# Order of products in an attention piece: both state products first, then eight quarter-width products

## The chip, the cores and the metric

The kernel runs on one core of a Trainium2 chip. The metric is the device time of one execution in microseconds (us). The kernel before takes 2143.31 us, the median of three runs (2138.61 to 2150.04). Five engines share the work: TensorE (products), VectorE, ScalarE and GpSimd (element-wise work), and SyncE (starts transfers).

## What is computed

Input x has 4 x 1024 tokens of 512 values. Two layers follow each other, each with a normalisation before and after and a sum with its input: a linear attention with decay (16 heads of 32 values, chunks of 128 tokens), and a mixture of 8 experts, 2 per token, with a shared expert. The change touches the attention only, and there the recurrence over chunks:

```python
def step(S, inp):
    qb, kb, vb = inp
    inter = jnp.einsum('bhcd,bhde->bhce', qb * decay_q[None, :, :, None], S)
    scores = jnp.einsum('bhcd,bhed->bhce', qb, kb) * dmask[None]
    intra = jnp.einsum('bhce,bhed->bhcd', scores, vb)
    S_new = lam_c[None, :, None, None] * S + jnp.einsum('bhcd,bhce->bhde', kb * decay_k[None, :, :, None], vb)
    return (S_new, inter + intra)
```

## The kernel before

Tokens are taken in 8 blocks of 512 (two blocks to a sequence), a block in 4 chunks of 128. The 16 heads stand in 4 groups of 4, so a group fills 128 partitions with 4 x 32 values. In each block the attention is a list of pieces with places on a scale (PLACES, OPENING): `QK` and `V` make q, k and v, `Z` (ScalarE) spreads q so that one product gives the scores of four heads, `S` (L741) makes the scores of one group and VectorE masks them into `probs` (L1122), `IP` makes inter + intra, `ST` (L759) the new state, `OUT` the projection.

`IP` is the piece of the change. It exists for each block, chunk and half (two groups), 8 x 4 x 2 = 64 times. For each of its groups it runs a state product, `state` x `qd`, with weights of 128 x 128 (L749), and four quarter-width products, one for each head, with the 128 x 32 weights `v` and the moving operand `probs`; each writes 32 partitions of the output bank (L753). All of it adds up in 256 columns of one PSUM bank, of which ScalarE (L938) and VectorE (L1127) make `attT_hi` and `attT_lo`. These products are plain f32. Large products elsewhere split each operand into a high and a low part and run three products (`three`, L678 to L680).

Block 0 runs its attention alone. From block 1 on, the pieces of attention are mixed with parts of the shared expert (`GA`, `UP`, `DN`) by a list that `schedule` makes: each engine has one fixed order (`ORDER`), and pieces wait for each other by counters (`p_piece`, `a_piece`, `v_piece`). The list holds whole pieces; inside a piece the order is that of the code. The attention ends at about 1290 us of the span; then come the experts and the last block.

Of the kernel before, what the change touches and what calls it, by code (L numbers as in the profile page):

```python
# [16 lines left out]
P = 128  # L17
# [300 lines left out]
def done(engine, *piece):  # L318

    return PLACE[engine][piece]  # L320
# [10 lines left out]
def build(nc, x, w_att, w_ffn, w_gu, w_dn, w_router, b_qk, b_v, b_out, t_mask, t_dq, t_dk, t_lam, t_blk, t_ident,  # L331
# [10 lines left out]
    with ExitStack() as ctx:  # L342
        def sb(name, shape, dt=F32, scope=ctx):
            return scope.enter_context(nc.sbuf_tensor(name, [P] + shape, dt))
# [67 lines left out]
        qd = sb("q_decayed", [G, P], scope=phase1)  # L412
        kd = sb("k_decayed", [D], scope=phase1)
        probs = sb("probsT", [2, GH, P], scope=phase1)
        state = sb("state", [G, P], scope=phase1)
# [186 lines left out]
        def w_landed(a, u):  # L602

            return 32 * ((a - 1) * (NW // WAS) + u // WAS + 1)
# [71 lines left out]
        def three(pe, out_ap, l_hi, l_lo, r_hi, r_lo, start, stop):  # L676

            pe.matmul(out_ap, l_hi, r_hi, start=start, stop=False)  # L678
            pe.matmul(out_ap, l_hi, r_lo, start=False, stop=False)  # L679
            return pe.matmul(out_ap, l_lo, r_hi, start=False, stop=stop)  # L680
# [11 lines left out]
        def pe_bank(pe, piece):  # L692

            old = bank_before(piece)
            if old:
                pe_evicted(pe, old)
            return bank_of(piece)

        def pe_attention(pe, piece):
            kind, a, *args = piece  # L700
            b = pe_bank(pe, piece)
            if kind in ("T1", "T2"):
                c, = args
                pe.wait_ge(a_piece, done("A", "N1", a, c) if kind == "T1" else done("A", "LX", a, c // 2))
                normed = xn2[:, c, 0:D] if kind == "T2" else xin[:, c, :]
                for k in range(KT):
                    mm = pe.transpose(b[:, k * P:(k + 1) * P], normed[:, k * P:(k + 1) * P], ident[:, :])  # L707
            elif kind == "QK":
                m, = args
                if a:  # L710
                    pe.wait_ge(wa_in[m % WAS], w_landed(a, m))
                else:
                    pe.wait_ge(v_piece, done("V", "W", a, m))
                if m == 0:
                    pe.wait_ge(v_piece, done("V", "T1", a, NC - 1))
                for k in range(KT):
                    ks = slice(k * P, (k + 1) * P)
                    mm = three(pe, b, wa_hi[:, m % WAS, ks], wa_lo[:, m % WAS, ks], xa_hi[:, k, :], xa_lo[:, k, :],
                               k == 0, k == KT - 1)
            elif kind == "V":  # L720
                c, = args
                cs = slice(c * P, (c + 1) * P)
                if c == 0:
                    if a:
                        for k in range(KT):
                            pe.wait_ge(wa_in[k], w_landed(a, 8 + k))
                    else:
                        pe.wait_ge(v_piece, done("V", "W", a, 11))
                for k in range(KT):
                    mm = three(pe, b, xa_hi[:, k, cs], xa_lo[:, k, cs], wa_hi[:, k, :], wa_lo[:, k, :],  # L730
                               k == 0, k == KT - 1)
            elif kind == "KT":
                c, = args
                if c == 0:
                    pe.wait_ge(a_piece, done("A", "QK", a, 7))
                for g in range(G):
                    mm = pe.transpose(b[:, g * P:(g + 1) * P], kT[:, g, c * P:(c + 1) * P], ident[:, :])
            elif kind == "S":
                c, g = args
                pe.wait_ge(a_piece, done("A", "Z", a, c, g))  # L740
                mm = pe.matmul(b, kT[:, g, c * P:(c + 1) * P], qz[:, g % 2].rearrange("p h t -> p (h t)"),  # L741
                               start=True, stop=True)
            elif kind == "IP":
                c, half = args
                pe.wait_ge(v_piece, max(done("V", "S", a, c, 2 * half + 1), done("V", "V", a, c), done("V", "KT", a, c)))
                for gl in range(2):
                    g = 2 * half + gl
                    cols = slice(gl * P, (gl + 1) * P)
                    pe.matmul(b[:, cols], state[:, g, :], qd[:, g, :], start=(gl == 0), stop=False,  # L749
                              skip_group_check=True)  # L750
                    for j in range(GH):
                        r = slice(j * HD, (j + 1) * HD)
                        mm = pe.matmul(b[r, cols], v[:, c, g * P + j * HD:g * P + (j + 1) * HD],  # L753
                                       probs[:, g % 2, j, :], start=False, stop=(gl == 1), skip_group_check=True)
            elif kind == "ST":
                c, = args
                for g in range(G):
                    gs = slice(g * P, (g + 1) * P)
                    mm = pe.matmul(b[:, gs], kd[:, gs], v[:, c, gs], start=True, stop=True)  # L759
            elif kind == "OUT":  # L760
                c, = args
                if c == 0:
                    if a:
                        for k in range(KT):
                            pe.wait_ge(wa_in[k], w_landed(a, 12 + k))
                    else:
                        pe.wait_ge(v_piece, done("V", "W", a, 15))
                pe.wait_ge(v_piece, done("V", "IP", a, c, 1))
                for k in range(KT):
                    mm = three(pe, b, oT_hi[:, k, :], oT_lo[:, k, :], wa_hi[:, k, :], wa_lo[:, k, :],  # L770
                               k == 0, k == KT - 1)
            elif kind == "R1":
                pe.wait_ge(v_piece, done("V", "T2", a, NC - 1))
                for k in range(KT):
                    ks = slice(k * R, k * R + P)
                    mm = three(pe, b, rw_hi[:, ks], rw_lo[:, ks], xs_hi[:, k, :], xs_lo[:, k, :],
                               k == 0, k == KT - 1)
            elif kind == "R2":
                pe.wait_ge(a_piece, done("A", "R1", a))
                for c in range(NC):  # L780
                    mm = pe.matmul(b[:, c * R:(c + 1) * R], lgT[0:R, c * P:(c + 1) * P], ident[0:R, 0:R],
                                   start=True, stop=True)
            elif kind == "RK":
                pe.wait_ge(v_piece, done("V", "CM", a))
                pe.matmul(b[:, 0:(NC + 1) * E], ones[:, :], before[:, :, :].rearrange("p c e -> p (c e)"),
                          start=True, stop=False)
                mm = pe.matmul(b[:, 0:NC * E], route[:, R_TRI:R_TRI + P], chosen[:, :, :].rearrange("p c e -> p (c e)"),
                               start=False, stop=True)
            mm.then_inc(p_piece, 1)
# [547 lines left out]
        @block.tensor  # L1337
        def _(pe):
            pe.wait_ge(const_in, 16 * N_CONST)
            for p in ORDER["P"]:  # L1340
                if p == ("R1", 0):
                    pe.wait_ge(const_v, 8)
                    pe.wait_ge(const_a, 1)
                if p[0] in ATT:
                    pe_attention(pe, p)
                elif p[0] in FFN:
                    pe_ffn(pe, *p)
                else:
                    pe_moe(pe, *p)
# [132 lines left out]
```

## Time and profile before

| | |
|---|---|
| median of the runs | 2143.31 us |
| profiled execution | 2150.83 us |
| its span | 2149.0 us |
| TensorE busy, products | 1991.3 us (93%) |
| TensorE busy, weight loads (beside products) | 1596.2 us (74%) |
| VectorE busy | 1204.6 us (56%) |
| ScalarE busy | 969.1 us (45%) |
| mean granted clock of TensorE | 0.972 |
| 190 to 1290 us (blocks 1 to 7 of attention, mixed) | TensorE 1046.01 of 1100 us, VectorE 626.96, ScalarE 443.40 |

In the rows, PE is TensorE's products, PEld its weight loads, DVE VectorE, ACT ScalarE, POOL GpSimd and SP SyncE. "banks<-q_decayed,state" is a product that writes `banks` and reads the other two; 128*32 behind it is the size of its weights. The ends of products are modelled, so their starts are the firmer numbers. Products overlap in the records, since the next one enters before the last has left.

### The profile page before, as it was taken

To read this page: it belongs to the slowest core of one execution; us is meant where nothing else is said; L and a number is where in the kernel's file an instruction comes from. 1 tells how busy PE (TensorE), PEld (TensorE's weight loads), DVE (VectorE), ACT (ScalarE), POOL (GpSimd) and SP (SyncE) were. 2 spreads that over 40 slices of the span, in tenths; PEclk is the share of its full clock that TensorE was granted. 3 is DMA by queue.
4 is the path that set the end of the run, shared out by engine and by line. 5 is a ranking of instruction groups with operands and counts; after the bars stand their busy time and mean duration, and the time that the engine had idled before them with its cause. 6 is when DMAs were issued, how large, how long until landed. Compare 5 with 4: busy or idle time off the path is not lost.

```text
span 2149.0 us, 28704 instructions
## 1 busy us (share of the span) xinstructions
PE 1991.3 (93%) x10192; PEld 1596.2 (74%) x10192; DVE 1204.6 (56%) x2878; ACT 969.1 (45%) x1942; POOL 370.3 (17%) x380
## 2 busy tenths in 40 slices
PE   6787999999989998999999999999999999999994
PEld 4465677777767776767767767777999999999873
DVE  3554664574655574575575556444666666666474
ACT  4332443443443443343354334334666666666452
POOL 2201001001001000100100100201333343333122
PEclk9888999999989999999999999999999999999997
DMA  7985235436236336426435434735899999988596
GB/s 243 359 293 197 92 111 201 159 111 213 97 127 216 111 106 219 142 79 208 156 106 189 133 111 142 250 106 192 225 250 245 246 246 246 245 246 240 137 247 103
DMA packets 145149, 394.53 MB, mean 184 GB/s; under 512 B 17168, under 2 KB 17328, under 8 KB 137840
## 3 DMA queue, kind: packets, MB, share of 16 engines
q0 software_dynamic: 45792, 189.60, 30.7%
q1 hardware_dynamic: 98784, 203.02, 29.4%
q8 instruction: 83, 1.36, 0.3%
q14 instruction: 58, 0.48, 0.1%
q10 hardware_dynamic: 432, 0.07, 0.0%
HBM read 283.96 MB, written 108.67 MB: 183 GB/s over the span
## 4 chain that ended last, share of the span: by engine, by line
PE 81%; DVE 7%; issue 4%; DMA 3%; ACT 2%; SPq 1%; POOL 1%; POOLq 0%; ACTq 0%; DVEq 0%
PE banks L678 23%; PE banks L680 22%; PE banks L679 22%; PE banks L741 4%; DMA xT_lo<-xt_scratch 2%; PE banks L749 2%; PE banks L753 2%; PE banks L853 2%; PE banks L759 1%; PE banks L859 1%; PE banks L707 1%; DVE probsT L1122 1%; DVE pair_stats L1060 1%; SPq L651 1%; POOL out L594 1%
## 5 line engine op out<-in xcount | busy, mean ns | idle before, releaser
L678 PE MATMUL banks<-xT_hi,ffn_gate_up_hi 128*128 128x512 f32 x704 | 303.0, 430 | 29.4 <-DMA xT_lo<-xt_scratch 22.0
L680 PE MATMUL banks<-xT_hi,ffn_gate_up_lo 128*128 128x512 f32 x704 | 282.0, 401 | 0.0
L679 PE MATMUL banks<-xT_lo,ffn_gate_up_hi 128*128 128x512 f32 x704 | 281.0, 399 | 0.0
L678 PE MATMUL banks<-moe_gu_hi,moe_xT_hi 128*128 128x352 f32 x624 | 216.3, 347 | 3.0 <-DVE moe_xT_lo L1281 3.0
L931 ACT COPY q_one_head<-qT 32x128 f32<-32x128 f32 x512 | 151.1, 295 | 119.6 <-PE banks L741 114.2
L680 PE MATMUL banks<-moe_gu_hi,moe_xT_lo 128*128 128x352 f32 x624 | 202.0, 324 | 0.0
L679 PE MATMUL banks<-moe_gu_lo,moe_xT_hi 128*128 128x352 f32 x624 | 201.1, 322 | 0.0
L678 PEld LDWEIGHTS banks<-xT_hi,ffn_gate_up_hi 128*128 128x128 f32 x704 | 135.9, 193 | 80.6 <-issue 22.2
L1274 DVE TENSOR_TENSOR moe_gu_lo<-moe_gu_raw,moe_gu_hi 128x704 fp32r<-128x704 f32 x156 | 135.1, 886 | 99.3 <-ACT moe_gu_hi L988 99.3
L586 POOL DMA_INDIRECT ffn_out<-moe_y,moe_x x78 | 125.3, 1607 | 282.8 <-ACT moe_y L1014 267.6
L679 PEld LDWEIGHTS banks<-xT_lo,ffn_gate_up_hi 128*128 128x128 f32 x704 | 136.3, 194 | 32.2 <-issue 7.4
L680 PEld LDWEIGHTS banks<-xT_hi,ffn_gate_up_lo 128*128 128x128 f32 x704 | 136.0, 193 | 30.8
L1257 DVE TENSOR_TENSOR ffn_gate_up_lo<-ffn_w_raw,ffn_gate_up_hi 128x768 fp32r<-128x768 f32 (+1 forms) x176 | 120.8, 686 | 61.7 <-ACT ffn_gate_up_hi L961 61.5
L938 ACT CAST attT_hi<-banks 128x256 fp32r<-128x256 f32 x64 | 23.7, 370 | 258.6 <-PE banks L753 258.5
L678 PE MATMUL banks<-ffn_down_hi,hidden_hi 128*128 128x512 f32 x308 | 133.6, 434 | 3.4 <-DVE hidden_lo L1267 3.4
L741 PE MATMUL banks<-q_one_head,kT 128*128 128x512 f32 x256 | 133.2, 614 | 0.7 <-ACT q_one_head L931 0.7
L1278 DVE TENSOR_TENSOR moe_dn_lo<-moe_dn_raw,moe_dn_hi 128x512 fp32r<-128x512 f32 x117 | 77.4, 688 | 90.9 <-ACT moe_dn_hi L994 90.8
L1122 DVE TENSOR_TENSOR probsT<-banks,decay_mask 128x512 f32<-128x512 f32 x128 | 87.4, 689 | 69.4 <-PE banks L741 67.5
L678 PEld LDWEIGHTS banks<-moe_gu_hi,moe_xT_hi 128*128 128x128 f32 x624 | 118.4, 190 | 6.8 <-DVE moe_xT_lo L1281 3.3
L531 POOL DMA_DIRECT2D out<-x x32 | 17.6, 553 | 610.1 <-DVE x_shift L1054 607.6
L679 PEld LDWEIGHTS banks<-moe_gu_lo,moe_xT_hi 128*128 128x128 f32 x624 | 119.2, 191 | 3.8
L680 PE MATMUL banks<-ffn_down_hi,hidden_lo 128*128 128x512 f32 x308 | 121.4, 394 | 0.0
(238 smaller groups left out, 4417.0 us busy)
## 6 DMA issues: line engine op xcount, KB each, us to landing
ffn_w_raw<-w_ffn SPq DMA_DIRECT2D x176, 384.0 KB, 3.2
att_w_hi<-att_w_split SPq DMA_DIRECT2D x112, 256.0 KB, 3.6
att_w_lo<-att_w_split SPq DMA_DIRECT2D x112, 256.0 KB, 4.5
x_normed_by_expert<-x_normed POOLq DMA_DIRECT2D x26, 771.0 KB, 17.5
moe_x<-x_normed_by_expert SPq DMA_DIRECT2D x78, 257.0 KB, 5.5
x_in<-x SPq DMA_DIRECT2D x32, 256.0 KB, 4.5
x<-x SPq DMA_DIRECT2D x32, 256.0 KB, 5.1
out<-x POOLq DMA_DIRECT2D x32, 256.0 KB, 2.7
```

The source lines that it names most:

```text
L586: pool.indirect_dma_start(out=acc_d[:, :], out_offset=bass.IndirectOffsetOnAxis(ap=xg[:, j % XG, D + 1:DX].bitcast(I32), axis=0), in_=y[:, ...
L678: pe.matmul(out_ap, l_hi, r_hi, start=start, stop=False)
L679: pe.matmul(out_ap, l_hi, r_lo, start=False, stop=False)
L680: return pe.matmul(out_ap, l_lo, r_hi, start=False, stop=stop)
L741: mm = pe.matmul(b, kT[:, g, c * P:(c + 1) * P], qz[:, g % 2].rearrange("p h t -> p (h t)"), start=True, stop=True)
L749: pe.matmul(b[:, cols], state[:, g, :], qd[:, g, :], start=(gl == 0), stop=False, skip_group_check=True)
L753: mm = pe.matmul(b[r, cols], v[:, c, g * P + j * HD:g * P + (j + 1) * HD], probs[:, g % 2, j, :], start=False, stop=(gl == 1), skip_group_ ...
L931: op = act.copy(qz[r, g % 2, j, :], qT[r, g, c * P:(c + 1) * P])
L1122: op = ve.tensor_tensor(probs[:, g % 2, :, :], chunked(b), mask[:, GH * g:GH * (g + 1), :], ALU.mult)
L1257: op = ve.tensor_tensor(wgu_lo[:, n % WGU, gu_cut], src, wgu_hi[:, n % WGU, gu_cut].bitcast(F32), ALU.subtract)
L1274: op = ve.tensor_tensor(gu_lo[:, i % 2, k, :], rgu[:, i % 2, k * GU:(k + 1) * GU], gu_hi[:, i % 2, k, :].bitcast(F32), ALU.subtract)
L1278: op = ve.tensor_tensor(dn_lo[:, i % 2, k, :], rdn[:, k * D:(k + 1) * D], dn_hi[:, i % 2, k, :].bitcast(F32), ALU.subtract)
```

## The change

In `IP` the loop over the two groups is split in two: the first runs both state products, the second both sets of four quarter products. The waits ahead of it and the counter behind it are the same.

```diff
                 for gl in range(2):
                     g = 2 * half + gl
+                    pe.matmul(b[:, gl * P:(gl + 1) * P], state[:, g, :], qd[:, g, :], start=(gl == 0), stop=False,
+                              skip_group_check=True)
+                for gl in range(2):
+                    g = 2 * half + gl
                     cols = slice(gl * P, (gl + 1) * P)
-                    pe.matmul(b[:, cols], state[:, g, :], qd[:, g, :], start=(gl == 0), stop=False,
-                              skip_group_check=True)
                     for j in range(GH):
                         r = slice(j * HD, (j + 1) * HD)
                         mm = pe.matmul(b[r, cols], v[:, c, g * P + j * HD:g * P + (j + 1) * HD],
```

## Rows read from the trace of the kernel before

**Rows 1.** The page: its span, and busy time of each engine.

```profile
span 2149.0 us, 28704 instructions
PE 1991.3 (93%) x10192; PEld 1596.2 (74%) x10192; DVE 1204.6 (56%) x2878; ACT 969.1 (45%) x1942; POOL 370.3 (17%) x380
```

**Rows 2.** The chain that ended last: shares by line; start us, us, what.

```profile
by line: PE banks L678 22.7%; PE banks L680 21.7%; PE banks L679 21.6%; PE banks L741 4.4%; issue 3.8%; DMA xT_lo<-xt_scratch 2.2%; PE banks L749 2.0%; PE banks L753 2.0%; PE banks L853 1.6%; PE banks L759 1.4%; PE banks L859 1.2%; PE banks
...
55.81 0.46 PE banks L749 x2
...
1284.86 0.36 PE banks L753 x8
```

**Rows 3.** Timeline of TensorE, one piece: start us, us, engine, line, operands, count.

```profile
576.57 0.40 PE L680 MATMUL banks<-xT_hi,ffn_gate_up_lo 128*128 128x512 f32 x1
576.80 0.27 PE L749 MATMUL banks<-q_decayed,state 128*128 128x128 f32 x1
576.91 0.28 PE L749 MATMUL banks<-q_decayed,state 128*128 128x128 f32 x1
577.12 0.32 PE L753 MATMUL banks<-probsT,v 128*32 128x128 f32 x4
577.25 0.29 PE L753 MATMUL banks<-probsT,v 128*32 128x128 f32 x4
577.47 0.38 PE L749 MATMUL banks<-q_decayed,state 128*128 128x128 f32 x1
577.89 0.42 PE L753 MATMUL banks<-probsT,v 128*32 128x128 f32 x8
578.25 0.50 PE L678 MATMUL banks<-xT_hi,ffn_gate_up_hi 128*128 128x512 f32 x1
```

**Rows 4.** Line 753: duration ns min/median/max, first and last start.

```profile
L753 PEld LDWEIGHTS banks<-probsT,v x1024: 106/109/155, 56.2 to 1285.6; 128*32 128x32 f32 x171
L753 PE MATMUL banks<-probsT,v x1024: 272/297/423, 56.2 to 1285.7; 128*32 128x128 f32 x171
```

**Rows 5.** Timeline of the weight loads of the same piece; idle time in brackets.

```profile
577.11 0.16 PEld L753 LDWEIGHTS banks<-probsT,v 128*32 128x32 f32 x8
577.47 0.30 PEld L749 LDWEIGHTS banks<-q_decayed,state 128*128 128x128 f32 x2 [0.20 <-issue]
```

**Rows 6.** Timeline of TensorE inside a state update.

```profile
591.75 0.50 PE L759 MATMUL banks<-v,k_decayed 128*128 128x128 f32 x3
```

**Rows 7.** The chain that ended last between 572 and 592 us.

```profile
574.23 0.69 DVE probsT L1122
...
589.57 0.46 PE banks L749 x2
```

**Rows 8.** Timeline at both ends of that stretch, with idle time before an instruction.

```profile
572.32 0.69 DVE L1136 TENSOR_TENSOR projected<-banks,bias_out 128x512 f32<-128x512 f32 x1 [1.50 <-PE banks L680]
573.18 0.69 DVE L1122 TENSOR_TENSOR probsT<-banks,decay_mask 128x512 f32<-128x512 f32 x1 [0.17 <-PE banks L741]
574.23 0.69 DVE L1122 TENSOR_TENSOR probsT<-banks,decay_mask 128x512 f32<-128x512 f32 x1 [0.36 <-PE banks L741]
...
589.57 0.46 PE L749 MATMUL banks<-q_decayed,state 128*128 128x128 f32 x2 [1.02 <-DVE probsT L1122]
```

**Rows 9.** Timeline of TensorE in a piece at the slower clock level.

```profile
269.73 0.66 PE L753 MATMUL banks<-probsT,v 128*32 128x128 f32 x8
269.95 0.44 PE L753 MATMUL banks<-probsT,v 128*32 128x128 f32 x4
...
271.05 0.66 PE L753 MATMUL banks<-probsT,v 128*32 128x128 f32 x8
```

**Rows 10.** TensorE's waits, 190 to 1290 us: total us, times, longest.

```profile
PE banks L678 <- DMA xT_lo<-xt_scratch: 11.5, 11, 3.1
PE banks L749 <- DVE probsT L1122: 10.7, 7, 3.8
```

**Rows 11.** Busy time behind a block's input load; then granted clock, DMA share, GB/s.

```profile
604.00:611.00 7.00, 6.45 (x15) 4.09 (x16) 0.53 (x1) 0.52 (x2) 0.00 (x0) 0.56 0.61 232
```

## The prediction

> **What bounds the kernel now.** I read the page first. TensorE is busy 93% of a span of 2149.0 us, VectorE 56% [rows 1], so TensorE's own row of work is the first candidate. The chain of waits says whether it really is: the two lines that the change touches, the state product (L749) and the quarter-width products (L753), stand in the chain that ended last with 2.0% and 2.0% of the span, together 86 us [rows 2]. That has to be set against what they take in all. One attention piece (one half of one chunk) goes from the start of its first product at 576.80 to the start of the next line's at 578.25, 1.44 us [rows 3], and there are 8 blocks x 4 chunks x 2 halves = 64 pieces, some 92 us plus what the slower clock adds. So about nine tenths of these pieces are on the path that sets the end. Going along the chain in windows of 100 us and looking for each piece gives the count: 56 of 64 are on it, the first at 55.81, the last with its quarter products at 1284.86 [rows 2], 8 are not. The eight stand where the chain runs through VectorE or through a load. [rows 7] show one of them: the chain leaves TensorE for a VectorE product at 574.23 and is back at 589.57, and the piece of 576.80 lies in between.
>
> **What one piece looks like now.** The view is the timeline in very narrow windows, so that single instructions come apart [rows 3]. An f32 product is executed as two instructions (1024 records for 512 quarter products [rows 4]), which I call passes. With starts in order: state product of the first group 576.80 and 576.91; its four quarter products in one go at 577.12, and their second pass at 577.25; state product of the second group from 577.47; its quarter products from 577.89; next line 578.25. Four products of quarter width start almost together (eight weight loads lie within 0.16 us [rows 5]), so a set of four costs one pass and not four.
>
> The steps are therefore:
> - full width to full width, same kind: 0.11 us (576.80 to 576.91);
> - full to quarter: 577.12 - 576.91 = 0.21;
> - quarter pass to quarter pass: 577.25 - 577.12 = 0.13;
> - quarter to full: 577.47 - 577.25 = 0.22, and from there 0.42 to the next quarter pass, where 0.11 + 0.21 = 0.32 would be due, so 0.10 more goes to the first full pass.
>
> **The change, part by part.** It removes no instruction and adds none; both state products go first, then eight quarter products. The wait ahead of the piece (the second group's masked scores, v, k transposed) is the same and was already ahead of everything in it, so no wait is added, moved or taken away, no DMA and no queue is passed. The order of additions per column stays.
>
> What goes: the stretch from the second pass of the first quarter set to the first pass of the second set, 577.89 - 577.25 = 0.64 us, and the quarter pass behind it, 0.13, is priced anew: 0.77 us in all.
> What comes in its place:
> - the second state product right behind the first: two more passes of full width, back to back. The state update (L759) is eight such passes; three of them, the first at 591.75, take 0.50 with a last one of about 0.28 [rows 6], so (0.50 - 0.28) / 2 = 0.11 each. Two passes: 0.22 us.
> - the third quarter pass directly behind the second, and the fourth behind the third. The trace of before has only first-to-second (0.13); there the record of the first pass is longer (0.32 for four with starts 0.02 apart) than that of the second (0.29), so it seems to wait 0.02 for its first load, and the ends of the two are 0.11 apart [rows 3]. Bounds: 0.13 each (as recorded by starts) and 0.107 each (a little under the steps of full passes, by their rounding). I take 0.11, because the third and fourth have their loads already under way as the second has. Two passes: 0.22 us.
> Saving per piece: 0.77 - 0.22 - 0.22 = 0.33 us; bounds 0.77 - 0.22 - 0.26 = 0.29 and 0.77 - 4 x 0.107 = 0.34. A piece at the slower clock level has steps of nearly double length: 271.05 - 269.95 = 1.10 from quarter pass to quarter pass across the state product, and 269.95 - 269.73 = 0.22 per pass [rows 9], which gives 1.10 + 0.22 - 4 x 0.22 = 0.44. Four pieces are like that, so 0.4 us more in all.
>
> How much of it reaches the end: 56 pieces on the chain x 0.33 = 18.5, plus 0.4 = 18.9 us. The other eight pieces only make a wait longer (the 1.02 us before 589.57 becomes 1.35 [rows 8]). Then there is the second chain next to the first. Where TensorE hands over to VectorE in that stretch, VectorE had been idle 1.50, 0.17 and 0.36 us before three operations, each time released by TensorE [rows 8], so about 2.0 us of slack stood against some 1.3 us (four pieces) saved since the chain was last pinned. That covers it, but narrowly: with the cover gone, one more piece in each of the seven interleaved blocks drops out, 7 x 0.33 = 2.3 us. I take half, 1.1. Outside the pieces TensorE's waits between 190 and 1290 us are small and nearly all set off by TensorE's own earlier products (11.5 us for the input load, 10.7 for masked scores [rows 10]); such waits move with it and keep their length. Behind 1290 us nothing changes. Saving: 18.9 - 1.1 = **17.8 us**.
>
> **From the profiled execution to the median.** The profiled execution took 2150.83 us with a span of 2149.0; the median of the runs is 2143.31, 7.5 us less. The saving is a sum of fixed steps, so I take it off both: 2133.0 for an execution like the profiled one, **2125.5 us** for the median, -0.83%.
>
> **A rule against this.** In the trace the loads for the second quarter pass are issued while the first pass is in flight: all eight loads fall into 0.16 us from 577.11, while the first products run until about 577.43, with weights of all 128 rows and 32 columns, as the forms in the records say [rows 3, 5]. The Trainium skill, page "TensorE: Matmul & The Clock Gate", Part 3, says that a weight load overlaps products in flight only where it addresses other rows of the array. By that rule the time would be that of rival (b) below, 2155 us; by the row it is the 2125.5 above. The same page, in Part 2, names a second case, a load into the background weights, and the trace agrees with that one. What no row shows is a third set behind the second.
>
> **The rivals.**
> (a) *VectorE or ScalarE takes over.* The gain is real on TensorE but the chain that bypasses it is nearer than I think, and only half of the pieces pass theirs on: 28 x 0.33 = 9.2 us, 2134 us. For it: the chain leaves TensorE for 15 us at a stretch in a block [rows 7]. Against it: 56 pieces on the chain, VectorE 56% busy. 0.13.
> (b) *Weights of the third and fourth quarter pass load in the open.* This one ends slower. If only one set of weights can be kept ready and the one behind it must wait until products in flight have ended, a pass costs the product (0.27) and a load (0.11), 0.38 us [rows 4], in place of 0.11. Both passes so: 0.77 - 0.22 - 0.76 = -0.21 us per piece, +11.8 us for 56, 2155 us. It decides from (0.77 - 0.22) / 2 = 0.28 us per pass upwards. If it strikes the third pass alone: 0.77 - 0.22 - 0.38 - 0.13 = 0.04, 2141 us. Against it: full passes run at 0.11 for eight in a row [rows 6], and nothing but their width differs. 0.04 for the first, 0.03 for the second.
> (c) *The clock.* TensorE arrives earlier at waits that it doesn't shorten, idles longer, and the granted clock falls more often. Behind a block's wait for its input load the stretch 604 to 611 us was granted 0.56, that is mostly the level of 1.2 instead of 2.4 GHz [rows 11]; 7 us at it cost about 3.5. Five more such stretches eat the gain: 2143 us. But a wait that grows does so by 0.33 us, against a longest of 3.1 for those loads and 3.8 for masked scores [rows 10]. 0.04.
> (d) *It does nothing.* If what costs 0.64 us were not the change of width but any change of operands, the step would remain: 2143 us. Against it: from L680 (a 512-wide product of another layer) to the state product there is no extra step, 576.57 to 576.80 [rows 3], as between products of that layer. 0.04.
>
> **How the numbers follow.** My forecast 0.72, (a) 0.13, (b) 0.07, (c) 0.04, (d) 0.04. The forecast's own range: 56 x 0.29 less 2.3 = 13.9, and 64 x 0.34 + 0.4 = 22.2 us, so 2129 to 2121; the three runs of before lie 11 us apart (a median of three can be 4 off), which makes 2116 to 2133. For 8 in 10 the range takes in (a) and most of (d) and (c): 2116 to 2141 us. About 0.5% (10.7 us) is what a measurement of this kernel can tell from no change. Faster by more: 0.72 of the forecast less a little at its edge, 0.71. Within: (a), one part of (b), (c), (d), 0.23. Slower: the rest of (b) and a tail of (c), 0.06.
>
> **What would show it.** In the changed kernel's timeline a piece should go full, full, full, full 0.11 apart, 0.21 to the first quarter pass, then 0.13, 0.11, 0.11, 0.22 to the next line: 1.11 us in place of 1.44. A third pass 0.3 us or more behind the second shows (b). A piece of 1.11 us with a time above 2133 shows (a) or (c): the waits of TensorE on masked scores and on v grown by over 2 us, or more stretches at the half level. The prediction would be wrong, with the piece right, if far fewer than 56 pieces passed their part on.

## The result and the profile after

The changed kernel takes 2127.97 us, the median of six runs (2123.69 to 2133.5); the kernel before, with three more runs beside them, 2145.16. The ratio is 0.992 with a 95% interval of 0.9903 to 0.9937: 17.2 us faster, 0.8%. The forecast was 2125.5 us and a saving of 17.8.

The page of the changed kernel, its span and the engines' busy time, which answer to [rows 1]:

```profile
span 2128.1 us, 28704 instructions
PE 1966.2 (92%) x10192; PEld 1593.7 (75%) x10192; DVE 1203.5 (57%) x2878; ACT 969.1 (46%) x1942; POOL 371.6 (17%) x380
```

The count of instructions is that of before, and TensorE's products are what moved: 25 us less busy time, against 2.5 for its weight loads and 1.1 for VectorE. The timeline of one piece (block 3, chunk 2, half 0, the one of [rows 3]), in windows narrow enough to separate passes, products first and then the weight loads:

```profile
569.68 0.40 PE L680 MATMUL banks<-xT_hi,ffn_gate_up_lo 128*128 128x512 f32 x1
569.91 0.27 PE L748 MATMUL banks<-q_decayed,state 128*128 128x128 f32 x1
570.02 0.50 PE L748 MATMUL banks<-q_decayed,state 128*128 128x128 f32 x3
570.25 0.28 PE L748 MATMUL banks<-q_decayed,state 128*128 128x128 f32 x1
570.45 0.32 PE L755 MATMUL banks<-probsT,v 128*32 128x128 f32 x4
570.58 0.51 PE L755 MATMUL banks<-probsT,v 128*32 128x128 f32 x12
570.80 0.29 PE L755 MATMUL banks<-probsT,v 128*32 128x128 f32 x4
571.02 0.50 PE L678 MATMUL banks<-xT_hi,ffn_gate_up_hi 128*128 128x512 f32 x1
...
570.45 0.38 PEld L755 LDWEIGHTS banks<-probsT,v 128*32 128x32 f32 x16
571.02 0.19 PEld L678 LDWEIGHTS banks<-xT_hi,ffn_gate_up_hi 128*128 128x128 f32 x1 [0.20 <-issue]
```

Four full passes go from 569.91 to 570.25, so 0.11 apart; 0.20 to the first quarter pass; the second at 570.58 (0.13) and the fourth at 570.80, so the third and fourth take 0.22 together, 0.11 each; 0.22 to the next line. The piece is 571.02 - 569.91 = 1.11 us, where it was 1.44. The sixteen quarter loads lie within 0.38 us. The first four, at 570.45, start together with the first quarter pass and not ahead of it; the other twelve, for the passes behind it, start while earlier quarter passes run. Then the loader idles 0.20 us before the first load of full width.

How the saving adds up is seen in the starts of the same pieces in both traces. First those of before, then those of after: the piece of block 0 after a long wait, the first piece of block 1, the piece behind VectorE's stretch in block 3, the last piece.

```profile
107.27 0.46 PE L749 MATMUL banks<-q_decayed,state 128*128 128x128 f32 x2 [1.79 <-DVE probsT L1122]
199.87 0.46 PE L749 MATMUL banks<-q_decayed,state 128*128 128x128 f32 x2 [0.88 <-DVE v L1110]
...
1284.48 0.38 PE L749 MATMUL banks<-q_decayed,state 128*128 128x128 f32 x2
```

```profile
106.93 0.55 PE L748 MATMUL banks<-q_decayed,state 128*128 128x128 f32 x1 [3.04 <-DVE probsT L1124]
199.01 0.57 PE L748 MATMUL banks<-q_decayed,state 128*128 128x128 f32 x3 [0.88 <-DVE v L1112]
...
582.68 0.68 PE L748 MATMUL banks<-q_decayed,state 128*128 128x128 f32 x4 [1.33 <-DVE probsT L1124]
...
1267.24 0.49 PE L748 MATMUL banks<-q_decayed,state 128*128 128x128 f32 x3
```

- Block 0: its 8 pieces bring the start of block 1 forward by 0.86 us only, or 1.22 if one counts from its first piece, which started 0.36 us later than before (56.17 and 55.81). At 106.93 the wait for masked scores has grown from 1.79 to 3.04 us.
- Blocks 1 to 7: from 199.87 to 1284.48 are 1084.61 us, from 199.01 to 1267.24 are 1068.23, 16.4 us less over 55 pieces, as much as 49 of them would give. Not all of it is theirs: within these stretches the clock records have TensorE at the slower level (1.2 GHz) for 34.1 us before and 30.7 after, which is up to 1.7 us. The rest, 14.7 us or more, is what 44 pieces give.
- The piece of 576.80 is one that was called off the chain. The wait behind it grew from 1.02 [rows 8] to 1.33 us, so its 0.31 us went there.
- The piece behind it (chunk 2, half 1) was counted on the chain, and in blocks 2 and 4, where both traces have the full clock there, it brings the next piece forward by 0.02 and 0.04 us only. Its gain goes into the wait of the transposes behind it (L707), which by the code need normalised rows from ScalarE; in block 2, before and after:

```profile
435.64 0.30 PE L707 MATMUL banks<-identity,x_normed 128*128 128x128 f32 x1 [0.28 <-issue]
430.81 0.30 PE L707 MATMUL banks<-identity,x_normed 128*128 128x128 f32 x1 [0.61 <-issue]
```

- At the last piece the kernel is 17.2 us ahead, the same number as between the medians. The profiled execution ends 20.9 us earlier, so 3.7 us more, in a part that the change doesn't touch.

Those 3.7 us are the clock's, in the main. From the last piece to TensorE's last product it is at the slower level for 27.3 us before and 16.0 after. One such place is in the stretches of 40 us that start some 195 us behind the last piece, before and after (granted clock is the third number from the end):

```profile
1480.00:1520.00 40.00, 35.49 (x185) 32.12 (x184) 16.95 (x27) 17.86 (x31) 8.45 (x9) 0.91 0.62 189
```

```profile
1462.00:1502.00 40.00, 35.48 (x200) 31.78 (x199) 17.17 (x28) 19.59 (x35) 9.21 (x10) 1.00 0.68 205
```

TensorE is equally busy in both, but does 15 products more in the second. A granted clock lower by 0.09 over 40 us is worth 3.6 us at the most. Followed product by product, the lead of the changed kernel grows by 2.6 us there, from 18.7 to 21.3; it gains and loses at other such places behind it.

The medians aren't free of it either. The runs of the kernel before beside the experiments (20) list a mean granted clock of 0.9738, the six of the changed kernel 0.9753. The difference of 0.0016 (before rounding) is up to 3.4 us of 2145, so of the 17.2 us some 14 to 17 come from the steps of the pieces. Six runs don't fix that closely, and whether the change of order brings the higher clock about isn't shown: the run with an extra product between the quarter sets, below, is the slowest of all and lists 0.9758.

### The profile page after: what moved, and what is told of

It is laid out like the page before. It is cut to its first block, busy times and chain, and to the rows that moved or that the text cites. A ratio compares the mean times of both kernels' runs of the same rounds, so it can differ in the third digit from the quotient of the medians.

```text
span 2128.1 us, 28704 instructions
## 1 busy us (share of the span) xinstructions
PE 1966.2 (92%) x10192; PEld 1593.7 (75%) x10192; DVE 1203.5 (57%) x2878; ACT 969.1 (46%) x1942; POOL 371.6 (17%) x380
## 4 chain that ended last, share of the span: by engine, by line
PE 58%; DVE 5%; issue 3%; DMA 2%; ACT 1%; POOL 1%; SPq 0%; POOLq 0%; ACTq 0%; DVEq 0%
PE banks L678 17%; PE banks L680 17%; PE banks L679 16%; PE banks L741 2%; PE banks L855 2%; PE banks L861 1%; DMA xT_lo<-xt_scratch 1%; POOL out L594 1%; PE banks L755 1%; PE banks L748 1%; PE banks L761 1%; DVE pair_stats L1062 1%; PE banks L707 0%; DVE probsT L1124 0%; DVE ffn_gate_up_lo L1259 0%
```

## Experiments

The theory: what costs is the change between weights of 128 and of 32 columns; each pair of changes (quarter to full and back) that is taken out of a piece saves 0.33 us, and TensorE's chain passes it to the end except where VectorE sets the pace. Rivals: it is the alternation of operands or groups, not the width; or the gain is taken up by a chain through VectorE or ScalarE. All runs stand against the kernel before, run on the same chip beside them.

### No change of width inside a piece, order of before

```diff
-                    pe.matmul(b[:, cols], state[:, g, :], qd[:, g, :], start=(gl == 0), stop=False,
-                              skip_group_check=True)
+                    for j in range(GH):
+                        r = slice(j * HD, (j + 1) * HD)
+                        pe.matmul(b[r, cols], state[:, g, r], qd[:, g, :], start=(gl == 0), stop=False,
+                                  skip_group_check=True)
                     for j in range(GH):
```

> Order of before (group by group), but each state product is made as four products of quarter width (32 columns of the state as weights, 32 partitions of the output), so no width changes inside a piece. If the 0.64 us step is the change of width: a piece takes about 1.11 us as in the changed kernel (0.21 in, seven steps of 0.11 to 0.13 between eight passes, 0.22 out), and the time falls by about 17 us against before, ratio 0.992. If it were the alternation of operands or of groups as such, the steps inside would stay near 0.2 to 0.4, a piece at 1.44 us or above, ratio 1.00. A third rival: 1024 more instructions cost something of their own, a piece between 1.2 and 1.44.

Measured: 2130.33 us against 2145.69, ratio 0.9937 (0.992 to 0.9954). The same piece in its timeline (L751 is the state product in four quarters, L755 the quarter products):

```profile
567.25 0.39 PE L680 MATMUL banks<-xT_hi,ffn_gate_up_lo 128*128 128x512 f32 x1
567.57 0.42 PE L751 MATMUL banks<-q_decayed,state 128*32 128x128 f32 x8
567.81 0.40 PE L755 MATMUL banks<-probsT,v 128*32 128x128 f32 x8
568.03 0.40 PE L751 MATMUL banks<-q_decayed,state 128*32 128x128 f32 x8
568.25 0.40 PE L755 MATMUL banks<-probsT,v 128*32 128x128 f32 x8
568.58 0.50 PE L678 MATMUL banks<-xT_hi,ffn_gate_up_hi 128*128 128x512 f32 x1
```

Operands and groups alternate as they did before, and yet each pair of passes takes 0.22 to 0.24 us. So the width it is. How much of a change is TensorE emptying and how much the late weight load, no run separates. The piece is 1.01 us and not 1.11, but that isn't a gain: the entry, 567.25 to 567.57, is 0.32 where it is 0.23 with a full product first (569.68 to 569.91), because the change of width now lies ahead of the piece. Both add to 1.33 or 1.34 us, and the times are alike: 15.4 and 17.2 us below before. The 768 additional records of products cost nothing that is seen: four quarters of a product go as one pass.

### The change of width put back, and its control

Both runs have the changed kernel's order and one more full-width product per piece, into columns that nobody reads. In the first it stands between the quarter sets:

```diff
                 for gl in range(2):
                     g = 2 * half + gl
                     cols = slice(gl * P, (gl + 1) * P)
+                    if gl:
+                        pe.matmul(b[:, 2 * P:3 * P], state[:, g, :], qd[:, g, :], start=False, stop=False,
+                                  skip_group_check=True)
                     for j in range(GH):
```

> Changed kernel, with one more full-width product per piece (a second state product of group 1 into columns nobody reads) between the two quarter sets. By the width theory that puts the step of 0.64 and 0.13 us back: piece 1.11 + 0.55 = 1.66 us, time about 12 us above before (64 pieces x 0.22, some hidden), ratio 1.005. If a change of width cost nothing and the gain came from elsewhere, it would add the two bare passes only: 1.33 us.

In the second it stands right behind the two state products:

```diff
                     pe.matmul(b[:, gl * P:(gl + 1) * P], state[:, g, :], qd[:, g, :], start=(gl == 0), stop=False,
                               skip_group_check=True)
+                pe.matmul(b[:, 2 * P:3 * P], state[:, g, :], qd[:, g, :], start=False, stop=False,
+                          skip_group_check=True)
```

> The same extra product and the same count of instructions as the run with it between the sets, but placed right behind the second state product. Width theory: two bare passes of 0.11, piece 1.33 us, time about 12 us above the changed kernel and 5 us below before, ratio 0.998; the difference to the run with the product between the sets is 0.33 us per piece, some 18 to 21 us. If placement doesn't matter, both runs are equal.

Measured: 2158.95 us, ratio 1.0059 (1.0041 to 1.0077), and 2139.17 us, ratio 0.9973 (0.9962 to 0.9984), against 2145.69 us of before beside them. The second piece of block 3 in the first and in the second kernel:

```profile
537.71 0.60 PE L748 MATMUL banks<-q_decayed,state 128*128 128x128 f32 x4
538.25 0.42 PE L758 MATMUL banks<-probsT,v 128*32 128x128 f32 x8
538.60 0.49 PE L754 MATMUL banks<-q_decayed,state 128*128 128x128 f32 x2
539.02 0.43 PE L758 MATMUL banks<-probsT,v 128*32 128x128 f32 x8
539.38 1.16 PE L764 MATMUL banks<-v,k_decayed 128*128 128x128 f32 x8
```

```profile
528.51 0.60 PE L748 MATMUL banks<-q_decayed,state 128*128 128x128 f32 x4
528.95 0.39 PE L750 MATMUL banks<-q_decayed,state 128*128 128x128 f32 x2
529.27 0.64 PE L757 MATMUL banks<-probsT,v 128*32 128x128 f32 x16
529.84 1.16 PE L763 MATMUL banks<-v,k_decayed 128*128 128x128 f32 x8
```

539.38 - 537.71 = 1.67 us against 529.84 - 528.51 = 1.33: with the same instructions, one pair of changes of width is 0.34 us, and the times differ by 19.8 us. For 64 pieces that is 0.31 each, so nearly all of it arrives. The clock has hardly a part in this difference: the runs list 0.9758 and 0.9753, and in the profiled executions both are at the slower level for 27.3 us between the first piece of block 1 and the last piece, where they come to lie 17.9 us further apart, 54 pieces' worth of 55. The control is 6.5 us below before where the changed kernel is 17.2 below, so its product costs some 10.7 us (12 expected), 0.22 us for about 49 pieces.

### Which pieces count

The changed kernel, with the same dose (five extra products) in blocks 1 to 7 in one piece each. The first run has it in chunk 2, half 0, which is off the chain in six of these blocks:

```diff
+                for _ in range(5 if a and (c, half) == (2, 0) else 0):
+                    pe.matmul(b[:, 2 * P:3 * P], state[:, g, :], qd[:, g, :], start=False, stop=False,
+                              skip_group_check=True)
```

> Changed kernel, with five extra full-width products beside the state products of chunk 2, half 0, in blocks 1 to 7 only: ten passes, 1.1 us per block. This is the piece whose 0.33 us only lengthened the wait of the next piece (1.02 to 1.34 us). If it is off the chain because VectorE sets the pace there, six of seven doses vanish in that wait: it shrinks to about 0.25 us, the next piece starts at the same place in its block, and the time grows by 0 to 2 us. If the piece is on the path after all, 7.7 us more.

The other run has (0, 1) in place of (2, 0), a piece on the chain.

> The same dose of 1.1 us per block in blocks 1 to 7, but in chunk 0, half 1, a piece that lies on the chain. If the chain as read is right, each block is 1.1 us longer and the time grows by 7 x 1.1 = 7.7 us over the changed kernel. If the gain of a piece is taken up by slack further on (the rival that VectorE or ScalarE takes over), less than half of that arrives.

Measured: 2129.01 us, ratio 0.9915 (0.9897 to 0.9932), and 2136.88 us, ratio 0.9944 (0.9925 to 0.9962), against 2147.24 of before beside them. The first is 18.2 us below before and the second 10.4, where the changed kernel is 17.2 below. So the first dose costs nothing that can be measured, and the second 6.8 us, or 7.9 against the first run. The dose in block 3 and the piece behind it, first off the chain:

```profile
569.28 1.28 PE L751 MATMUL banks<-q_decayed,state 128*128 128x128 f32 x10
...
581.65 0.68 PE L748 MATMUL banks<-q_decayed,state 128*128 128x128 f32 x4 [0.31 <-DVE probsT L1127]
```

and on it:

```profile
531.33 1.28 PE L751 MATMUL banks<-q_decayed,state 128*128 128x128 f32 x10
...
586.93 0.68 PE L748 MATMUL banks<-q_decayed,state 128*128 128x128 f32 x4 [1.38 <-DVE probsT L1127]
```

In the first the wait is 0.31 us where it was 1.33: 1.02 of the 1.1 us are swallowed by it. In the second that wait is as it was, and the dose has gone through to the end. So for these two pieces the chain of waits, read before the change, named rightly which counts, and the slack there is small, 1.3 us per block. It isn't exact to a third of a microsecond: the piece of chunk 2, half 1, stands in the chain of before and yet passed next to nothing on in blocks 2 and 4.

### State products ahead of the wait

The two state products don't need the masked scores, for which a piece waits. In the changed kernel's order the wait can be split:

```diff
-                pe.wait_ge(v_piece, max(done("V", "S", a, c, 2 * half + 1), done("V", "V", a, c), done("V", "KT", a, c)))
+                pe.wait_ge(v_piece, done("V", "KT", a, c))
                 for gl in range(2):
                     g = 2 * half + gl
                     pe.matmul(b[:, gl * P:(gl + 1) * P], state[:, g, :], qd[:, g, :], start=(gl == 0), stop=False,
                               skip_group_check=True)
+                pe.wait_ge(v_piece, max(done("V", "S", a, c, 2 * half + 1), done("V", "V", a, c), done("V", "KT", a, c)))
                 for gl in range(2):
```

> Changed kernel, with the wait of the piece split: the state products wait for the transposed k and decayed q alone, and run ahead of the wait for masked scores and v, which only the quarter products need. Some 22 pieces stand idle 0.87 us or more ahead of their first product; in these four passes (0.11 each, and the slower start, 0.44 to 0.55 us) go into the idle time. If those waits lie on the path that sets the end, 22 x 0.5 = 11 us less than the changed kernel, about 2117 us, ratio 0.987. If the clock is lost in turn, or the pieces' waits are on a chain through VectorE that has slack elsewhere, 0 to 5 us.

Measured: 2116.63 us (2115.65 to 2117.95), ratio 0.9867 (0.9851 to 0.9883), 29.1 us below before (2145.69 beside it), where the changed kernel is 17.2 below: 11.9 us more, with 11 expected. This version beats both. Up to 2 us of the 11.9 can be the clock, whose mean is 0.9763 in these four runs and 0.9753 in the changed kernel's. TensorE's waits of 1 us and more in total, for masked scores and v, in the changed kernel:

```profile
PE banks L748 <- DVE probsT L1124: 30.6, 13, 5.1
PE banks L748 <- DVE v L1112: 8.1, 8, 1.4
```

and in this one (L748 the state products, L756 the quarter products):

```profile
PE banks L756 <- DVE probsT L1125: 14.4, 6, 4.4
PE banks L748 <- DVE probsT L1125: 7.9, 6, 3.4
PE banks L756 <- DVE v L1113: 2.0, 6, 0.3
```

38.7 us of waits have become 24.3. The profiled execution gains by the clock as well: between the first piece of block 1 and the last piece TensorE is at the slower level for 20.5 us, where it was 30.7 in the changed kernel's. Six waits stayed ahead of the state products, put down to masked scores. A state product doesn't read them. Its output bank does: with attention mixed in, its pieces share two banks, and by the code the bank of these six pieces (chunk 2, half 1) held the scores of the group before last, so it is free when VectorE has read them. That is argued from the code; no run took this wait away.

## Why the prediction was right

- **The steps of a piece.** The term that no row of before showed, the third and fourth quarter pass, was taken as 0.11 each with 0.13 as the other end; it is 0.11 each. Two full passes more: 0.22, as taken from the state update. Saving 0.33 as said, the same at the full clock in pieces that start at once (1.44 to 1.11 us) and in those behind a wait (1.52 to 1.19). At the slower level it is 0.46 (2.60 to 2.14), where 0.44 was forecast.
- **Reason for it.** The width theory was argued from three rows of before. The run without changes inside a piece (1.01 us plus a dearer entry) and the pair with the extra product (1.67 and 1.33 us) show it.
- **How much arrives.** 56 pieces and a loss of 1.1 us to a second chain were forecast. In blocks 1 to 7, 47 of 55 were counted on the chain; with the clock's part 49 pieces' worth came and without it 44. So a loss of the size that was taken fits, and the pieces of chunk 2, half 1, in blocks 2 and 4 show one. It lies at another place than was said, though: not where TensorE hands over to VectorE but at the transposes behind VectorE's stretch. In block 0 it was less: all eight pieces were counted, some 3 us with those at the slower clock, and 1.2 came.
- **What took it in block 0.** The chain of before runs through those pieces but with waits for VectorE between them, and the clock moved. Here are the same 2.3 us of the span, shortly ahead of the wait that grew, before and after (busy time of TensorE's products is the first number behind the length, granted clock the third from the end):

```profile
102.70:105.00 2.30, 2.30 (x4) 0.67 (x2) 1.95 (x12) 0.33 (x1) 0.55 (x1) 0.51 1.10 256
102.70:105.00 2.30, 1.19 (x3) 0.19 (x1) 1.92 (x13) 0.00 (x0) 1.67 (x3) 1.00 1.03 379
```

  With the clock of 1.00 in place of 0.51 TensorE comes to the wait at 103.89 and not at 105.48 us, but the masked scores come only 0.34 us earlier. Behind the longer wait the clock is at the slower level (0.50 from 106.1 to 108.3 us, where it was 1.00), so the piece takes 2.13 us and not 1.75.
- **Luck in the number.** The forecast of 17.8 us was made from steps alone. Block 0 gave nearly 2 us less than was counted, and a higher granted clock, which the forecast had only as a danger, gave up to 3.4 back in the medians. That 17.8 and 17.2 lie so close is in part that; the mechanism alone is good for 14 to 17.
- **(a) VectorE takes over**: at the piece beside its stretch, and (by the code) ScalarE at the piece behind it in blocks 2 and 4; far from half of the pieces. The dose off the chain shows the first and its bound.
- **(b) Loads in the open**: refuted by third and fourth passes 0.11 us behind the one ahead, where it needed 0.28, and by sixteen loads within 0.38 us. All address the same 128 rows, and products run meanwhile. The Trainium skill's sentence in "TensorE: Matmul & The Clock Gate", Part 3, that a load overlaps products in flight only on other rows, doesn't hold here; its second case in Part 2, a load into background weights, fits the passes within one width, though no run shows such a buffer itself.
- **(c) The clock**: it moved, but in the other direction than the rival had it, in the profiled executions and, by up to 3.4 us, in the medians.
- **(d) It does nothing**: refuted by the time, and its reason, that any change of operands costs the step, by the run with all products at quarter width.
- **From the profile to the median.** The forecast took 7.5 us off the profiled execution of before to get at its median; with three more runs that median is 2145.16, and the distance 5.7 us. Of the changed kernel the profiled execution is 1.9 us above the median. The difference of the two, 3.8 us, is about the 3.7 us of the clock. A small slip in its range: 2121 less 4 is 2117, not 2116; nothing hangs on it.

## What to carry to other kernels

Where TensorE alternates between weights of full width and of quarter width, sort the products so that each width comes once: a pair of changes costs 0.33 us at a granted clock of 1.00 (2.4 GHz), three full f32 passes of this size. Look at single passes before pricing such a change, since a merged row hides where the step is; then count on the chain of waits which repetitions pay, as those ahead of a wait for another engine give nothing. Once products are sorted, the ones put first may need less than the wait ahead of them asks for: moving that wait behind them brought two thirds as much again as the sorting. And a gain of less than 1% wants the granted clock of all runs beside it, since a small shift there is worth some of it.

## What the runs showed of the hardware

- Entering quarter width costs 0.20 instead of 0.11 us from pass to pass; leaving it costs 0.20 to 0.22 to the first full pass and 0.10 more to the next. The Trainium skill's page "TensorEngine Tiling (Array Packing)", Key Properties, says that changing the tiling mode drains the engine, without a price. The trace agrees so far as the steps on both sides of a change are dearer by these amounts.
- A full product split into four quarter-width products takes the same time as the full one, once the engine is at that width: 0.22 us for two passes of either kind. Four products of a set start 0.02 us apart in all.
- Within a run of quarter-width passes each pass's weight loads start while products of the same rows and columns are running: for the second to fourth pass of a piece, and in the run with all products at quarter width for the second to eighth. The loads of the first pass behind a change of width aren't pulled ahead.
